# A decoder layer with a selective scan: products and scans over two state columns per instruction

## What is computed

```python
proj = einsum('blh,he->bel', x, W_in); hidden, gate = split(proj, 2, axis=1)      # 1024 channels each
hidden = silu(causal_conv4(hidden) + conv_bias)
dt, Bm, Cm = split(einsum('ble,ed->bld', hidden^T, W_x), [128, 144])               # 16 states
dts = softplus(dt @ W_dt + b_dt)
dA = exp(dts[..., None] * A);  dBu = dts[..., None] * Bm[:, :, None, :] * hidden^T[..., None]
state = dA * state + dBu  (over the 512 steps);   y = sum_n state * Cm
out = ((y + hidden * D) * silu(gate)) @ W_out
```

## Time and profile before

| | before |
|---|---|
| median of 3 runs | 1273.64 us (1269.49 to 1277.2) |
| span of the profiled execution | 1267.2 us |
| the profiled execution's own device time | not among the numbers shown; the median is 6.4 us above the span |
| VectorE (DVE) busy | 1147.9 us, 1543 instructions |
| TensorE (PE) busy | 967.0 us |
| GpSimd (POOL) busy | 819.1 us |
| ScalarE (ACT) busy | 712.5 us |
| first unit starts / last unit ends | 71 / 1212 us |

### The profile page before, as it was taken

How to read it: one execution, slowest core, us unless ns; L and a number is a source line. 1 busy time by engine, 2 the same in 40 slices (tenths; PEclk the granted TensorE clock), 3 DMA queues, 4 the chain that set the end, 5 groups by cost and what they waited for, 6 DMA issues and landing times.

```text
span 1267.2 us, 11250 instructions
## 1 busy us (share of the span) xinstructions
PE 967.0 (76%) x2772; PEld 350.3 (28%) x2782; DVE 1147.9 (91%) x1543; ACT 712.5 (56%) x1082; POOL 819.1 (65%) x513
## 2 busy tenths in 40 slices
PE   7836777877799788767689779678689759664894
PEld 3211222221233233322133223222123223221342
DVE  3469999999999999999999999999999999979757
ACT  2566566647645664656656647565764656553232
POOL 2238777786876656767777566667777667655333
PEclk9956888778799768888789878778689778776897
DMA  5241222217811211115731111121951311131000
GB/s 164 62 123 50 55 54 59 79 26 181 220 34 42 58 42 50 50 54 124 218 102 50 51 48 53 33 71 53 220 137 36 110 39 41 34 97 36 17 0 34
DMA packets 63233, 95.23 MB, mean 75 GB/s; under 512 B 12736, under 2 KB 19008, under 8 KB 63168
## 3 DMA queue, kind: packets, MB, share of 16 engines
q1 hardware_dynamic: 37872, 60.85, 17.3%
q10 hardware_dynamic: 25296, 33.66, 10.7%
HBM read 56.46 MB, written 4.46 MB: 48 GB/s over the span
## 4 chain that ended last, share of the span: by engine, by line
DVE 51%; issue 26%; PE 17%; ACT 3%; DMA 2%; ACTq 1%; POOL 0%; DVEq 0%; SPq 0%; POOLq 0%
DVE st L728 31%; PE dense L831 12%; DVE dBu L723 5%; DVE ta L699 4%; DVE small L681 2%; DVE stats L688 2%; PE y_acc L873 2%; PE du_rep L859 1%; DMA dt_rep<-dts 1%; ACTq L550 1%; DVE x L803 1%; DVE hs L709 1%; PE dBu L841 1%; DVE dense L814 1%; DVE xsc L781 1%
## 5 line engine op out<-in xcount | busy, mean ns | idle before, releaser
L435 POOL TENSOR_TENSOR st<-st,Cb 128x1024 f32<-128x1024 f32 x250 | 587.8, 2359 | 276.8 <-DVE st L728 258.3
L728 DVE TENSOR_TENSOR_SCAN st<-dA,dBu 128x512 f32<-128x512 f32 x512 | 594.4, 1202 | 5.1 <-ACT dA L561 5.1
L561 ACT ACTIVATE dA<-dt_rep,Aneg 128x511 f32<-128x511 f32 x512 | 337.1, 711 | 165.8 <-DVE st L728 103.6
L723 DVE TENSOR_TENSOR dBu<-du_rep,Bb 128x512 f32<-128x512 f32 x500 | 319.6, 686 | 32.8 <-PE du_rep L859 26.9
L831 PE MATMUL dense<-xTs,Win 128*128 128x512 f32 x512 | 279.3, 697 | 42.1 <-ACTq L656 14.1
L859 PE MATMUL du_rep<-du,sel 32*128 32x512 f32 x256 | 168.3, 747 | 104.4 <-DVE dBu L723 104.3
L831 PEld LDWEIGHTS dense<-xTs,Win 128*128 128x128 f32 x512 | 111.3, 226 | 206.8 <-issue 206.4
L831 PE MATMUL dense<-wide,hs 128*128 128x512 f32 x256 | 119.3, 620 | 14.3 <-DVEq L817 8.7
L873 PE MATMUL y_acc<-st,sel 128*32 128x512 f32 x1024 | 124.3, 629 | 0.0
L859 PEld LDWEIGHTS du_rep<-du,sel 32*128 32x128 f32 x256 | 43.0, 212 | 216.6 <-issue 214.9
L699 DVE SCALAR_TENSOR_TENSOR ta<-dense,ck,ta 128x511 f32<-128x511 f32 (+2 forms) x96 | 71.6, 746 | 29.4 <-ACT ta L520 26.9
(11 more groups left out here) (107 smaller groups left out, 990.5 us busy)
## 6 DMA issues: line engine op xcount, KB each, us to landing
dt_rep<-dts ACTq DMA_DIRECT2D x512, 64.0 KB, 2.1
Win<-w_in SPq DMA_DIRECT2D x64, 256.0 KB, 2.6
wide<-w_out SPq DMA_DIRECT2D x4, 2048.0 KB, 10.3
wide<-bc_rows SPq DMA_DIRECT2D x24, 256.0 KB, 6.7
xTs<-xT SPq DMA_DIRECT2D x4, 1024.0 KB, 10.9
Bb<-bc_rows SPq DMA_DIRECT2D x16, 256.0 KB, 5.0
Cb<-bc_rows SPq DMA_DIRECT2D x16, 256.0 KB, 5.9
x<-x SPq DMA_DIRECT2D x3, 1024.0 KB, 6.0
```

Of the source, the lines that this page charges most:

```text
L435: nc.gpsimd.tensor_tensor(s, s, C[:, 2 * h:2 * h + 2, :], ALU.mult).then_inc(s_p, 1)
L561: nc.scalar.activation(dA[:, u % 2, j, 1:T], dt_rep[:, u % REPS, 1:T], ACT.Exp, scale=Aneg[:, u % UNITS, j:j + 1]).then_inc(s_dA, 1)
L723: V.tensor_tensor(dBu[:, j % 2, :], du_rep[u % 2][:], B[:, j, :], ALU.mult).then_inc(s_mul, 1)
L728: V.tensor_tensor_scan(st[:, u % RING, j, :], dA[:, u % 2, j, :], dBu[:, j % 2, :], 0.0, ALU.mult, ALU.add).then_inc(s_scan, 1)
```

## The change

Each unit now has two products and two scans, over two state columns (1024) each, in the order product, product, scan, scan. dBu has four banks, so a unit's products go to banks of their own; du_rep has one, and its spread waits for the second product of the unit before. The state sum is an item of its own, y, last in its step, and takes its bank in the ring of three. The tables are rearranged: the h keys are at steps 9, 10, 13, 14, 17, 18, 21, 22; z at g % 4 == 2 and ahead of h in its step; a gate at g % 4 == 3, in its own tile's last step; `finish` at g % 4 == 1; and REST anew. The core of the diff:

```diff
+NH = 2
+JH = NJ // NH
@@ tables
-REST = {"wo": [4, 5, 6, 8], "q": [1], "k": [3], "en": [9, 9, 12, 13], "at": [12, 13, 14, 15],
-        "xt": [14, 16, 17, 21], "av": [16, 18, 20, 22], "qt": [20, 22, 23, 26], "ff": [21, 24, 25, 27]}
+REST = {"wo": [2, 5, 6, 7], "q": [1], "k": [3], "en": [8, 9, 11, 12], "at": [10, 11, 13, 14],
+        "xt": [13, 14, 16, 18], "av": [15, 17, 19, 21], "qt": [18, 20, 22, 24], "ff": [19, 21, 23, 25]}
-HID_AT = [8, 10, 12, 14, 16, 18, 20, 22]
+HID_AT = [9, 10, 13, 14, 17, 18, 21, 22]
-Z_AT = 3
-GATE_AT = 1
+Z_AT = 2
+GATE_AT = 3
-FINISH_AT = 2
+FINISH_AT = 1
@@ items()
         rest(b - 1, table, ("wo", "q", "k", "at", "en"))
+    if (g % 4 == Z_AT and 0 <= n + 2 < NB * NE and n != -1) or (b, g) == (-1, 28):
+        keys.append(("z", (n + 2) // NE, (n + 2) % NE))
     if after and g in HID_AT:
         keys.append(("h", b + 1, HID_AT.index(g)))
...
-    if (g % 4 == GATE_AT and 0 <= n - 1 < NB * NE - 1) or (b, g) == (NB, 0):
-        keys.append(("g", (n - 1) // NE, (n - 1) % NE))
-    if (g % 4 == Z_AT and 0 <= n + 2 < NB * NE and n != -1) or (b, g) == (-1, 28):
-        keys.append(("z", (n + 2) // NE, (n + 2) % NE))
+    if g % 4 == GATE_AT and 0 <= n < NB * NE:
+        keys.append(("g", n // NE, n % NE))
...
+    if g % 4 == SUM_AT and 0 <= n - 1 < NB * NE:
+        keys.append(("y", (n - 1) // NE, (n - 1) % NE))
@@ PSUM
-        y_acc = ctx.enter_context(nc.psum_tensor("y_acc", [P, 512], F32))
-        du_rep = [ctx.enter_context(nc.psum_tensor(f"du_rep{i}", [P, 512], F32)) for i in range(2)]
-        dBu = ctx.enter_context(nc.psum_tensor("dBu", [P, 2, 512], F32))
+        du_rep = ctx.enter_context(nc.psum_tensor("du_rep", [P, 512], F32))
+        dBu = ctx.enter_context(nc.psum_tensor("dBu", [P, NJ, 512], F32))
@@ exps() on ScalarE
-                    act.wait_ge(s_scan, NJ * (u - 2) + j + 1)
+                    act.wait_ge(s_scan, NH * (u - 2) + j // JH + 1)
@@ finish() on VectorE
-                dve.wait_ge(s_ys, n + 1)
-                dve.wait_ge(s_gate, n + 1)
-                V.tensor_tensor(hs[:, b % 2, e, :], y_acc[:], ta[:, temp[("g", b, e)] % 2, :],
+                ps, free = full(("y", b, e))
+                dve.wait_ge(s_gate, NE * b + e + 1)
+                V.tensor_tensor(hs[:, b % 2, e, :], ps, ta[:, temp[("g", b, e)] % 2, :],
                                 ALU.mult).then_inc(s_y, 1)
+                dve.wait_ge(s_y, NE * b + e + 1)
+                dve.sem_inc(free, 1)
@@ unit() on VectorE
-                for j0 in range(0, NJ, 2):
-                    for j in (j0, j0 + 1):
-                        if u or j0:
-                            dve.wait_ge(s_scan, NJ * u + j - 1)
-                        V.tensor_tensor(dBu[:, j % 2, :], du_rep[u % 2][:], B[:, j, :],
-                                        ALU.mult).then_inc(s_mul, 1)
-                    for j in (j0, j0 + 1):
-                        dve.wait_ge(s_mul, NJ * u + j + 1)
-                        dve.wait_ge(s_dA, NJ * u + j + 1)
-                        V.tensor_tensor_scan(st[:, u % RING, j, :], dA[:, u % 2, j, :], dBu[:, j % 2, :], 0.0,
-                                             ALU.mult, ALU.add).then_inc(s_scan, 1)
+                for h in range(NH):
+                    j = slice(JH * h, JH * h + JH)
+                    if u:
+                        dve.wait_ge(s_scan, NH * (u - 1) + h + 1)
+                    V.tensor_tensor(dBu[:, j, :], du_rep[:].unsqueeze(1).to_broadcast([P, JH, T]), B[:, j, :],
+                                    ALU.mult).then_inc(s_mul, 1)
+                for h in range(NH):
+                    j = slice(JH * h, JH * h + JH)
+                    dve.wait_ge(s_mul, NH * u + h + 1)
+                    dve.wait_ge(s_dA, NJ * u + JH * (h + 1))
+                    V.tensor_tensor_scan(st[:, u % RING, j, :].rearrange("p j t -> p (j t)"),
+                                         dA[:, u % 2, j, :].rearrange("p j t -> p (j t)"),
+                                         dBu[:, j, :].rearrange("p j t -> p (j t)"), 0.0,
+                                         ALU.mult, ALU.add).then_inc(s_scan, 1)
@@ spread() on TensorE
-                if u >= 2:
-                    pe.wait_ge(s_mul, NJ * (u - 1))
-                nc.tensor.matmul(du_rep[u % 2][:], sel[rows, :], du[rows, n % 3, :], start=True,
+                if u:
+                    pe.wait_ge(s_mul, NH * u)
+                nc.tensor.matmul(du_rep[:], sel[rows, :], du[rows, n % 3, :], start=True,
                                  stop=True).then_inc(s_duf, 1)
@@ state_sum() on TensorE, now called from the items
-                if n:
-                    pe.wait_ge(s_y, n)
+                ps, done = bank_of(("y", b, e))
```

More of the change, by code:

```diff
@@ L251, in decoder_layer @@
         s_p = sem("cs_done")
-        s_ys = sem("y_summed")
         s_dd = sem("d_on_diagonal")
@@ L366, in _ @@
                 if b >= 1 and g == STAGED - 1 and b <= LAST:
-                    sp.wait_ge(s_mul, NJ * (UNITS * b + STAGED))
-                    sp.wait_ge(s_p, 2 * (UNITS * b + STAGED))
+                    sp.wait_ge(s_mul, NH * (UNITS * b + STAGED))
+                    sp.wait_ge(s_p, NH * (UNITS * b + STAGED))
                     load_w_out()
@@ L400, in _ @@
                         if b >= 0:
-                            sp.wait_ge((s_mul, s_p)[c], (NJ, 2)[c] * UNITS * (b + 1))
+                            sp.wait_ge((s_mul, s_p)[c], NH * UNITS * (b + 1))
                         elif c == 1:
@@ L431, in _ @@
                     C = spread_at(pool, u, s_cc, 1, Cb)
[L432 to L435, removed]
+                    for h in range(NH):
+                        pool.wait_ge(s_scan, NH * u + h + 1)
+                        j = slice(JH * h, JH * h + JH)
+                        s = st[:, u % RING, j, :]
+                        nc.gpsimd.tensor_tensor(s, s, C[:, j, :], ALU.mult).then_inc(s_p, 1)
                 for kb, i in pending:
@@ L601, in _ @@
                     if n + 1:
-                        act.wait_ge(s_ys, n + 1)
+                        product_done(act, ("y", n // NE, n % NE))
                     nc.scalar.activation(Ddiag[:], ident[:], ACT.Identity, scale=Dsk[:, (n + 1) % NE:(n + 1) % NE + 1]
@@ L704, in finish @@
             def finish(b, e):
-                n = NE * b + e
-                dve.wait_ge(s_ys, n + 1)
-                dve.wait_ge(s_gate, n + 1)
-                V.tensor_tensor(hs[:, b % 2, e, :], y_acc[:], ta[:, temp[("g", b, e)] % 2, :],
+                ps, free = full(("y", b, e))
+                dve.wait_ge(s_gate, NE * b + e + 1)
+                V.tensor_tensor(hs[:, b % 2, e, :], ps, ta[:, temp[("g", b, e)] % 2, :],
                                 ALU.mult).then_inc(s_y, 1)
+                dve.wait_ge(s_y, NE * b + e + 1)
+                dve.sem_inc(free, 1)
             def unit(u):
@@ L715, in unit @@
                 if u >= RING:
-                    dve.wait_ge(s_ys, (u - RING) // 4 + 1)
-                for j0 in range(0, NJ, 2):
-                    for j in (j0, j0 + 1):
-                        if u or j0:
-                            dve.wait_ge(s_scan, NJ * u + j - 1)
-                        V.tensor_tensor(dBu[:, j % 2, :], du_rep[u % 2][:], B[:, j, :],
-                                        ALU.mult).then_inc(s_mul, 1)
-                    for j in (j0, j0 + 1):
-                        dve.wait_ge(s_mul, NJ * u + j + 1)
-                        dve.wait_ge(s_dA, NJ * u + j + 1)
-                        V.tensor_tensor_scan(st[:, u % RING, j, :], dA[:, u % 2, j, :], dBu[:, j % 2, :], 0.0,
-                                             ALU.mult, ALU.add).then_inc(s_scan, 1)
+                    n = (u - RING) // NQ
+                    product_done(dve, ("y", n // NE, n % NE))
+                for h in range(NH):
[4 more added lines that the diff above has]
+                                    ALU.mult).then_inc(s_mul, 1)
+                for h in range(NH):
+                    j = slice(JH * h, JH * h + JH)
+                    dve.wait_ge(s_mul, NH * u + h + 1)
[4 more added lines that the diff above has]
+                                         ALU.mult, ALU.add).then_inc(s_scan, 1)
             def quantize_weight():
@@ L856, in spread, with state_sum @@
                 pe.wait_ge(s_du, n + 1)
-                if u >= 2:
-                    pe.wait_ge(s_mul, NJ * (u - 1))
-                nc.tensor.matmul(du_rep[u % 2][:], sel[rows, :], du[rows, n % 3, :], start=True,
+                if u:
+                    pe.wait_ge(s_mul, NH * u)
+                nc.tensor.matmul(du_rep[:], sel[rows, :], du[rows, n % 3, :], start=True,
                                  stop=True).then_inc(s_duf, 1)
-            def state_sum(n):
-                if n:
-                    pe.wait_ge(s_y, n)
+            def state_sum(b, e):
+                n = NE * b + e
+                ps, done = bank_of(("y", b, e))
                 pe.wait_ge(s_dd, n + 1)
```

(11 more changed lines are left out.)

## The result

| | before | changed |
|---|---|---|
| median device time | 1273.99 us (4 runs) | 1323.11 us (1317.44 to 1325.95, 4 runs) |
| span of the profiled execution | 1267.2 us | 1322.4 us (its own time 1324.19) |
| ratio of the times | | 1.0393, 95% interval 1.0358 to 1.0428 |

The change makes the kernel slower by 3.9%, 49 us. The forecast had the sign and its largest term, but 29.5 us in place of 49, and 1323 lies just above its range (1271 to 1322). The two profiled spans differ by 55.2 us, 6 more than the medians.

A forecast was written before the change was run, and what follows sets the result against it. VectorE, busy for 91% of the span, was taken as the bound. The terms -31 + 55 + 8 - 3.5 - 3 + 4 = +29.5 us, added to the median of 1273.64, gave about 1303 us, range 1271 to 1322.

The forecast's parts named there:

- Merged instructions, -31: VectorE's products and scans: four instructions less per unit, 128 units, 0.06 us each, so -31 us; bounds 0 and -77.
- Temp ring, +55: Two-slot ta/tb ring: VectorE waits up to 4.9 us before each pair's second h, +55 us; bounds 0 and 64.
- step 10's cover: Second and third batches: VectorE's other work at step 10 covers part of the slot wait, leaving 3.0 us.
- W_out's first product, +8: wo0 moved from step 4 to 2: VectorE waits 2.8 us in three batches, +8 us; bounds 0 and 15.
- Gate off step 25, -3.5: First batch: the gate moves to step 23, cutting VectorE's 4.61 us wait for a spread, -3.5 us.
- The step-5 waits: Second and third batches: the new table parts wo and gate, removing VectorE's 1.39 us waits for a spread, -3 us.
- One du bank, +4: PE cannot spread two units ahead; step 20 has 1.8 us of slack; +4 us, bounds 0 and 25.
- slots in time: Rival, chance 0.10: the second h's first term never waits for a ta/tb slot, time 1248 us.
- partly covered: Rival, chance 0.08: the slot wait is paid in the first batch only, time 1268 us, no change.
- the merge that saves nothing: Rival, chance 0.04: two banks in one VectorE instruction cost a restart, time 1334 us.
- the whole recorded time saved: Rival, chance 0.02: the merge saves 77 us instead of 31 on VectorE, time 1257 us.
- TensorE tied to VectorE: Rival, chance 0.08: the du bank and the ring of three cost 25 us rather than 4, time 1324 us.

The follow-up runs named there:

- experiments 3 and 11: Each merged 1024-column product and scan made two of 512 again: 3 in the changed kernel, 1340.1 us; 11 in the best version, 1265.7 us.
- Experiments 2: The changed kernel with the h keys two steps apart, at 9, 11, 13 to 23: 1281.8 us.
- experiment 5: The kernel before with only the h keys moved, to steps 9, 10, 13, 14, 17, 18, 21, 22: 1318.4 us.
- experiment 7: The changed kernel with wo0 at step 3 instead of 2: 1331.5 us.
- experiment 6: The kernel before with one du_rep bank in place of two, a spread waiting for all products of the unit before: 1336.9 us.
- experiment 1: The changed kernel with SyncE's loads of the next batch's B and C put before step 31's `load_w`: 1307.0 us.
- experiment 9: The changed kernel with SyncE's gate loads of steps 27 and 31 moved to the next step's end, and bc before z in step 26: 1297.8 us.
- the best version: The changed kernel with the order edits of experiment 9, h at steps 7, 9, 11 to 21, wo0 at step 3, k at step 2: 1238.9 us.

## Why the prediction was right and wrong

- **Merged instructions, -31:** right as work. 0.22 us a unit, 28 us; undone, it costs 27 to 28 us of VectorE's busy time in experiments 3 and 11 once the scalings are set aside. In time both show less of it, 17 and 22 us.
- **Temp ring, +55:** right in place, number and size: 12 pieces of 4.45 to 4.80 us, 56.8 in all. Only step 10's cover was too kind (4.45 left, 3.0 forecast). Experiments 2 and 5 show it from both sides.
- **W_out's first product, +8:** right, 8.6 us, and 0.9 three times for dA right behind it. The finish decides, as forecast: it ends at 364.6, wo0 begins at 364.74 and takes 9.8 us at a granted clock of 0.72. W_out now needs 16.1 to 17.3 us to land, not 10.3, and was there 0.8 to 2.1 us before. That one can move it for free was my later belief, and experiment 7 took it away.
- **Gate off step 25, -3.5:** gave 1.3 (waits of 0.72 and 2.57 in place of 4.61): the second stands behind the gate now at step 27, whose product took 5.57 us. The step-5 waits went as said.
- **One du bank, +4:** right in size, not in place. Waits for spreads after the start are 16.5 us before and 17.5 after, and 4.4 of the old ones went with the gate, so some 5 are new. Most lie in the last batch (12.2 us in three pieces after 1200 us of the span, against 8.3 in three pieces in the kernel before), which I had put at 0, and none at step 20 of the two batches before it, where I had looked. What I believed afterwards, that TensorE's lead is little used, is wrong (experiment 6).
- **The step that failed:** I followed the gate to steps 27 and 31 only for what TensorE and VectorE do there. SyncE goes through the same steps, and each gate brings a `load_w` that waits for the gate's own product: the one of step 27 stands ahead of the store of B and C, the one of step 31 ahead of B's load. The sum has no term for it. I even counted z's place before the copy of B and C for the start-up alone. Cost 23.1 us of waits; 16 us came back in time by step 31 alone (experiment 1), and 22 to 25 with the gate of step 27 and bc moved too (experiment 9).
- **Not foreseen, the other way:** VectorE's scalings (TENSOR_SCALAR over 512 columns) got shorter, together 12 us. Two groups of the changed kernel (count | busy us, mean ns of one | idle us before):

```profile
L684 DVE TENSOR_SCALAR small<-x,xinv 128x512 f32<-128x512 f32 x12 | 16.0, 1336 | 0.4
L782 DVE TENSOR_SCALAR small<-small,rsum 128x512 f32<-128x512 f32 x12 | 14.6, 1220 | 0.4
```

  In the earlier trace rows they took 1652 and 1788. The reason is when they start beside GpSimd's products (see the last section), and that shifts with the tables and with the merge: the first group takes 1336 ns in the changed kernel and 1236 with the merge undone, but 1051 in the best version and 1625 with the merge undone there. With the h keys alone moved (experiment 5) it takes 1549 and the second group 1922.

So +55.2 us of span are 89.3 us more of idle time (56.8 slots, 23.1 B, 8.6 wo, the rest small) less 34.1 of busy time. Merge and scalings would be 40; 6 us of that I can't place. The rivals: slots in time, partly covered, the merge that saves nothing and the whole recorded time saved (the starts are 1.12 and 2.19 apart) are refuted. TensorE tied to VectorE was put at 1324, but that this is the measured time is luck: waits for spreads in the middle are 5 us, not 20. It is not the cause of the 49 us, but it is a limit on each repair. The range was drawn for errors in terms that I had, not for one that I had left out.

## What to carry to other kernels

When an item of a hand-written order moves, walk it through every engine's program, the DMA queue's too: list what each one does for it in the new step, what that waits for, and what stands behind it. A ring of two slots over keys of several kinds gives a release distance in steps, and it has to be read off the new order key by key; two uses in neighbouring steps can cost the whole chain through the slowest giver. Giving up a double buffer cost 5% here under one table and left few waits under another, so the two are changed and judged together.

## What was unexpected of the hardware

- A 1024-column product or scan on VectorE, its output or input in two PSUM banks, costs no more than two of 512 and saves about one start: 1.12 and 2.19 us apart, against 2 x 0.59 and 2 x 1.12. The recorded durations, 1221 and 2269 ns, are again longer than the distance of the starts. The Trainium skill (VectorE: DVE Perf Modes, "The DRAIN you can't avoid") says that the next operation does not start until the pipe is empty, and also that one that is not held starts earlier; the trace shows the second, 0.08 to 0.10 us before the recorded end.
- A scaling of 512 columns took 486 ns by itself and up to 2.6 us beside GpSimd's products. Kernel before, GpSimd and then VectorE:

```profile
416.48 4.68 POOL L435 TENSOR_TENSOR st<-st,Cb 128x1024 f32<-128x1024 f32 x2
450.52 2.34 POOL L435 TENSOR_TENSOR st<-st,Cb 128x1024 f32<-128x1024 f32 x1 [1.06 <-DVE st L728]
```

```profile
419.41 2.03 DVE L775 TENSOR_SCALAR small<-small,rsum 128x512 f32<-128x512 f32 x1
421.54 0.49 DVE L775 TENSOR_SCALAR small<-small,rsum 128x512 f32<-128x512 f32 x1
450.53 2.61 DVE L775 TENSOR_SCALAR small<-small,rsum 128x512 f32<-128x512 f32 x1
```

  The first ends 0.28 us after GpSimd's pair, the third 0.28 after its product, and the second, with GpSimd idle, takes 0.49. So it is with all 25 of 36 in the kernel before that last over 0.5 us: each ends 0.28 to 0.29 us after the end of a GpSimd instruction that it overlapped. The scaling is held until GpSimd is through, and what it costs depends on how far that product has come. The Trainium skill (SBUF — State Buffer, "SBUF: two separate sides") says that GpSimd and a VectorE instruction in a 2-port mode take a shared pair of ports by turns, each for its whole instruction. No row shows the mode of these scalings; the ends agree with taking turns. The 12 us gained by a mere shift of phase show what it can cost here.
- The loads of B and C, the staged ones among them, of 256 KB each, landed in 3.6 to 13.3 us (median 7.2) in the changed kernel.
